# All pieces of the gated layer's weights rounded in the first attention, none in the rotary attention

## The reference, cut to what matters

```python
def nf4_quant_dequant(w):
    flat = w.reshape(-1, 64)
    absmax = jnp.max(jnp.abs(flat), axis=1, keepdims=True)
    normalized = flat / jnp.where(absmax == 0, 1.0, absmax)
    bounds = (NF4_CODE[:-1] + NF4_CODE[1:]) * 0.5
    return (NF4_CODE[jnp.searchsorted(bounds, normalized)] * absmax).reshape(w.shape)
x = x + L0_xattn(norm(x)) ; x = x + L0_ffn(norm(x)) ; ... ; x = x + L2_xattn(norm(x))
h = silu(x @ nf4(w1).T) * (x @ nf4(w2).T) ; x = x + h @ nf4(w3).T    # on norm(x)
```

## Time and profile before

| | before |
|---|---|
| median of 3 runs | 3158.59 us (3151.64 to 3164.6) |
| the profiled execution's own time | 3164.61 us |
| its span | 3162.1 us |
| mean granted TensorE clock | 0.956 |
| busy: TensorE, VectorE, ScalarE, GpSimd | 91%, 63%, 43%, 42% |

### The profile page before, as it was taken

How to read it: one execution, slowest core, us unless ns; L and a number is a source line. 1 busy time by engine, 2 the same in 40 slices (tenths; PEclk the granted TensorE clock), 3 DMA queues, 4 the chain that set the end, 5 groups by cost and what they waited for, 6 DMA issues and landing times. The chain is left out here.

```text
span 3162.1 us, 44768 instructions
## 1 busy us (share of the span) xinstructions
PE 2887.2 (91%) x16404; PEld 2486.6 (79%) x16404; DVE 2001.8 (63%) x3496; ACT 1369.1 (43%) x3381; POOL 1317.0 (42%) x1174
## 2 busy tenths in 40 slices
PE   7999999999876984789999998998999999999967
PEld 6888888888764762578888886887999999999955
DVE  5777777777855777668888875344444444444453
ACT  3656565565611552134444433213444444443520
POOL 6455535554422651455555550003434434443430
PEclk9999999999977996899999999998999999999978
DMA  3112112111121000211111102101000100000000
GB/s 129 49 57 66 58 41 66 60 51 59 39 80 45 11 4 7 70 47 41 44 41 44 32 27 104 51 11 37 28 21 24 31 18 28 28 28 18 18 28 27
DMA packets 77831, 131.85 MB, mean 42 GB/s; under 512 B 10024, under 2 KB 23600, under 8 KB 77232
## 3 DMA queue, kind: packets, MB, share of 16 engines
q1 hardware_dynamic: 68112, 112.10, 11.2%
q10 hardware_dynamic: 9504, 16.91, 1.7%
HBM read 114.23 MB, written 14.75 MB: 41 GB/s over the span
## 5 line engine op out<-in xcount | busy, mean ns | idle before, releaser
L89 PE MATMUL a_pa<-a_wo,a_ot 128*128 128x512 f32 x2304 | 538.5, 391 | 10.4 <-issue 7.5
L89 PEld LDWEIGHTS a_pa<-a_wo,a_ot 128*128 128x128 f32 x2304 | 429.6, 188 | 105.9 <-issue 13.1
L359 DVE SCALAR_TENSOR_TENSOR a_nf_acc<-a_nf_t,a_nf_acc 128x512 f32<-128x512 bf16 (+1 forms) x462 | 403.1, 872 | 46.3 <-ACT a_nf_t L313 15.7
L313 ACT ACTIVATE a_nf_t<-a_nf_w,a_nf_shifts 128x512 bf16<-128x512 f32 (+1 forms) x495 | 321.9, 709 | 178.7 <-DVE a_nf_w L343 149.3
L89 PE MATMUL a_pa<-h_t,a_wqk 128*128 128x512 f32 x1536 | 374.7, 396 | 1.7 <-DVE h_t L770 1.7
L89 PEld LDWEIGHTS a_pa<-h_t,a_wqk 128*128 128x128 f32 x1536 | 283.0, 189 | 56.8 <-DVE h_t L770 1.9
L89 PE MATMUL a_pa<-a_wv,ctx_t 128*128 128x512 f32 x960 | 232.3, 400 | 39.8 <-POOL a_wv L1617 23.9
L89 PEld LDWEIGHTS a_pa<-a_wv,ctx_t 128*128 128x128 f32 x960 | 182.3, 193 | 78.4 <-POOL a_wv L1617 24.8
L89 PE MATMUL a_pa<-ctx_t,a_wqk 128*128 128x512 f32 x960 | 224.5, 390 | 1.2 <-POOL a_wqk L1617 1.0
L89 PEld LDWEIGHTS a_pa<-ctx_t,a_wqk 128*128 128x128 f32 x960 | 179.8, 188 | 39.5 <-POOL a_wqk L1617 2.4
L1006 POOL TENSOR_TENSOR a_prob<-a_prob,a_inv 128x512 f32<-128x512 f32 x128 | 130.6, 1042 | 183.3 <-DVE a_inv L1372 183.3
(11 more groups left out here) (361 smaller groups left out, 6138.5 us busy)
## 6 DMA issues: line engine op xcount, KB each, us to landing
a_raw<-in_a_w SPq DMA_DIRECT2D x288, 256.0 KB, 2.6
a_nf_w<-in_nf ACTq DMA_DIRECT2D x32, 256.0 KB, 2.7
nf_rounded<-a_nf_acc ACTq DMA_DIRECT2D x32, 256.0 KB, 2.0
f_rows<-nf_rounded SPq DMA_DIRECT2D x22, 256.0 KB, 3.0
ctx_kept<-ctx_t SPq DMA_DIRECT2D x1, 4096.0 KB, 17.0
ctx_t<-ctx_kept SPq DMA_DIRECT2D x1, 4096.0 KB
f_cols<-nf_rounded SPq DMA_DIRECT2D x11, 256.0 KB, 3.7
a_ctx_raw<-in_ctxt SPq DMA_DIRECT2D x4, 512.0 KB, 6.8
```

Source lines behind the costliest of these rows:

```text
L89: ins = nc.tensor.matmul(out, lhs(a), rhs(b), start=first and i == 0, stop=last and i == 2)
L313: self.nc.scalar.activation(self.t[:, m % NF4_RING, cols], self.w[:, p % 2, cols], ACT.Identity, bias=self.shifts[:, u - 2:u - 1], scale=s ...
L359: ins = nc.vector.scalar_tensor_tensor(acc, t, c, acc, inner, outer)
```

## The change

`NF4_SIZES` has all 33 pieces and goes to the first attention; the quotas there grow by four units a head on VectorE, and on ScalarE by one after each of the four kept halves. In the rotary attention every trace of the rounding goes: its tiles, its 15 memsets on GpSimd, its loads and stores in ScalarE's queue and its units.

```diff
@@ -236,9 +236,8 @@
 NF4_BLOCKS = 3 * NH2 * D // (P * NF4_BLOCK)
 NF4_UNITS = 18
 NF4_RING = 4
-SIZES0 = [8] * 24
-SIZES2 = [8] * 8 + [2]
-assert sum(SIZES0) + sum(SIZES2) == NF4_BLOCKS
+NF4_SIZES = [8] * 32 + [2]
+assert sum(NF4_SIZES) == NF4_BLOCKS
 
 
 def counted(keys):
@@ -754,9 +753,9 @@
                 if h + 2 < H:
                     for key in (("q", h + 2, 0), ("q", h + 2, 1), ("k", h + 2, 0)):
                         keep(key)
-                        rounding.on_scalar(act, 3 if h % 2 == 0 else 2)
+                        rounding.on_scalar(act, 4 if h % 2 == 0 else 3)
                     keep(("k", h + 2, 1))
-                    rounding.on_scalar(act, 2 if h % 2 == 0 else 6)
+                    rounding.on_scalar(act, 3 if h % 2 == 0 else 7)
             rounding.on_scalar(act, NF4_UNITS * len(rounding.sizes))
             rounding.finish(act)
 
@@ -842,7 +841,7 @@
                     inverse(h + 1, 1)
                 rest_of_o(h, 0)
                 rest_of_o(h, 1)
-                rounding.on_vector(dve, 10 if h % 2 else 13)
+                rounding.on_vector(dve, 14 if h % 2 else 17)
                 for key in bias_outputs(h):
                     add_output(*key)
                     if key[1] % 2:
@@ -1492,7 +1491,7 @@
     return order
 
 
-def rope_attention_stage(nc, x, ident, ctx_t, h_t, where, pieces_in, mask_in, pos_in, iota_in, tables_in, nf4):
+def rope_attention_stage(nc, x, ident, ctx_t, h_t, where, pieces_in, mask_in, pos_in, iota_in, tables_in):
 
 
     st = Stage(nc, "a2")
@@ -1541,7 +1540,6 @@
     top, shift, total, inv = (next_at(n, [P, NB]) for n in ("top", "shift", "total", "inv"))
     space = next_at("space", [P, 11 * NB])
     iota = next_at("iota", [P, DC])
-    rounding = Rounding(nc, st, next_at, *nf4)
 
     pa = st.ps("pa", [P, ROPE_RING, BANK])
     pscore = st.ps("pscore", [P, 2, BANK])
@@ -1567,9 +1565,6 @@
 
     def bank(key):
         return pa[:, (made_count[key] - 1) % ROPE_RING, :]
-
-    def side(step):
-        return (2, 1, 2) if step < 14 else (2, 0, 2)
 
     with nc.Block() as block:
         @block.sync
@@ -1636,7 +1631,6 @@
             norm.rstd_on_gpsimd(nc, pool)
             split(("k", 0))
             split(("k", 1))
-            rounding.set_up_on_gpsimd()
             nc.gpsimd.tensor_scalar(ident_bf[:, :], ident[:, :], 1.0, 0.0, ALU.mult, ALU.add).then_inc(mask_set, 1)
             pool.wait_ge(mask_loaded, 16)
             nc.gpsimd.tensor_scalar(neg[:, :, :], mask[:, :, :], 0.0, NEG, ALU.is_equal, ALU.mult).then_inc(mask_set, 1)
@@ -1827,18 +1821,13 @@
 
             for b in range(NB):
                 keep_values(0, b)
-            act.wait_ge(rounding.shifts_set, 15)
-            rounding.load(act, 0)
-            rounding.load(act, 1)
             for b in range(NB):
                 act.wait_ge(hp_ready, b + 1)
                 nc.scalar.activation(h_t[:, HI, :, b * P:(b + 1) * P], ph[b % 4], ACT.Copy).then_inc(h_hi, 1)
             for b in range(NB):
                 keep_values(1, b)
-                rounding.on_scalar(act, 3)
             exps(0, 0)
             exps(0, 1)
-            rounding.on_scalar(act, side(0)[0])
             for h in range(H):
                 for t in range(2):
                     act.wait_ge(t_ready, 2 * h + t + 1)
@@ -1852,9 +1841,6 @@
                     nc.scalar.activation(ot[:, h % 3, HI, t * BANK:(t + 1) * BANK], ptv[:, t, :], ACT.Copy).then_inc(o_hi, 1)
                 if h + 1 < H:
                     exps(h + 1, 1)
-                rounding.on_scalar(act, sum(side(h)[1:]) + side(h + 1)[0])
-            rounding.on_scalar(act, NF4_UNITS * len(rounding.sizes))
-            rounding.finish(act)
 
         @block.vector
         def _(dve):
@@ -1939,7 +1925,6 @@
             for n in range(1, 4):
                 rotate("k", n, 0)
                 rotate("k", n, 1)
-            rounding.on_vector(dve, 3 * NB)
             for key in (("k", 4), ("k", 5), ("k", 6), ("q", 0), ("k", 7)):
                 rotate(*key, 0)
                 rotate(*key, 1)
@@ -1953,7 +1938,6 @@
                 if h + 1 < H:
                     shifts(h + 1, 0)
                     shifts(h + 1, 1)
-                rounding.on_vector(dve, side(h)[0])
                 if h + 1 < H:
                     inverse(h + 1, 0)
                 if h + 2 < H:
@@ -1962,15 +1946,12 @@
                 rest_of_o(h, 1)
                 if h + 1 < H:
                     inverse(h + 1, 1)
-                rounding.on_vector(dve, side(h)[1])
                 if h + 2 < H:
                     rotate("q", h + 2, 1)
                 for key in rope_outputs(h):
                     add_output(*key)
-                rounding.on_vector(dve, side(h)[2])
             for key in rope_outputs(H):
                 add_output(*key)
-            rounding.on_vector(dve, NF4_UNITS * len(rounding.sizes))
             dve.wait_ge(a_taken, taken_count["o", H // 2 - 1, NB - 1])
     st.close()
 
@@ -3246,7 +3227,7 @@
         free_at = ht_at + 2 * DC * NT * 4
         with nc.sbuf_tensor("h_t0", [P, 2, DC, NT], F32R) as h_t:
             bias_attention_stage(nc, x, ident, ctx_t, h_t, free_at, ins["x"], ins["ident"], ins["ctxt"], ins["a0_w"],
-                                 ins["mask_bool"], ins["pos_bias"], ins["ln_w"], (ins["nf4"], rounded, 0, SIZES0))
+                                 ins["mask_bool"], ins["pos_bias"], ins["ln_w"], (ins["nf4"], rounded, 0, NF4_SIZES))
             ffn0_stage(nc, x, ident, h_t, ins["w_base"], ins["f0_side"], ins["lora_b"], ins["b_base"], ins["b_router"],
                        ctx_t, ctx_kept)
         patch_attention_stage(nc, x, ident, ins["ctx"], ins["mask_f"], ins["a1_wqk"], ins["a1_wv"], ins["a1_wo"],
@@ -3265,8 +3246,7 @@
                 ffn1_stage(nc, x, h, ident_bf, ins["f1_w"], ins["f1_scale"], ins["f1_bias"])
         with nc.sbuf_tensor("h_t1", [P, 2, DC, NT], F32R) as h_t:
             rope_attention_stage(nc, x, ident, ctx_t, h_t, (ctx_at, ht_at, free_at), ins["a2_w"], ins["mask_i"], ins["pos"],
-                                 ins["iota"], ins["rope"],
-                                 (ins["nf4"], rounded, sum(SIZES0), SIZES2))
+                                 ins["iota"], ins["rope"])
             ffn2_stage(nc, x, ident, h_t, rounded_rows, ctx_t, ctx_kept)
             latent_attention_stage(nc, x, ident, ctx_t, h_t, free_at, ins["a3_w"], ins["a3_norm"])
             ffn3_stage(nc, x, ident, h_t, ins["f3_a"], ins["f3_b"], ins["f3_router"], ins["f3_keys"])
```

## The result

| | before | after |
|---|---|---|
| median | 3161.44 us (3151.64 to 3164.6, 4 runs) | 3278.15 us (3272.7 to 3279.29, 4 runs) |
| ratio | | 1.0369, 95% interval 1.0353 to 1.0386 |
| span, mean granted clock | 3162.1 us, 0.956 | 3277.2 us, 0.943 |

The kernel became 3.7% slower. The forecast of 3238 us had the sign and the place right, and was 40 us short; the time lies 6 us above its range. Lines of the kernel after are one lower than before in the first attention (the scores are L632, the keeps L700).

What follows compares the result with a forecast made beforehand. The prediction took TensorE to bound the kernel before and VectorE the first attention's heads after. +68 +21 -10 = +79 on 3164.6 us gave 3243.6, less 6.0 for the median 3238 us; range 3188 to 3272 (80%).

Steps and rivals of the forecast that it cites:

- (a): VectorE's rounding in the first attention: a unit costs 0.77 us undisturbed, 0.965 in an even head, 1.31 beside `wv` splits.
- (b): First attention's heads: VectorE's own length makes a pair 59.0 us against 54.1; 13 pairs and head 0 give +68.
- (c): Even heads' scores wait 1.5 to 7 us for ScalarE's late keep of `k`; this pays (b), adding nothing.
- (d): End of the first attention: units left after head 29 delay `rest_of_o(31)`, the last additions and the last store, +21.
- (e): Rotary attention: waits freed by taking its rounding out, -10, bounds 0 and -28.
- The checks named beforehand: Heads: pair near 59 us, VectorE 85% or more, TensorE under 92%; rotary heads 15.8 us, VectorE near 65%.
- Rival 1: VectorE's spare quarter takes all added units, the pair stays 54.1 and the rotary stage gives 28: 3141 us, 4%.
- Rival 2: Milder: the additions' idle time and smoother rhythm take most, a pair grows 1.5 to 2 us: 3193 us, 18%.
- Rival 4: The work moves and nothing is seen, time within 16 us: 4%.
- Rival 3: Late keeps in even heads and bank waits in odd ones add, with half clock behind them: +114, 3273 us, 20%.
- SBUF: two separate sides: If the shared ports lock exclusively, added units cost 0.77 us each where GpSimd rests; sum some 25 us less.

Runs made afterwards that it cites:

- experiment 3: Kernel before with other piece counts, first plus rotary attention: 28 + 4.25 took 3220.9 us, 24 + 0 took 3147.8, 20 + 0 took 3121.8 (pair 52.6).
- keep first: Kernel after, with ScalarE's rounding units from between the two halves of `k` put behind the second half: 3276.7 us.
- experiment 1: ScalarE's rounding units between the halves of `k` moved behind the second half: 3276.7 us in the kernel after, 3155.6 us in the kernel before.
- experiment 2: Unused filler matmuls in TensorE's waits: kernel after, at the scores, 12 took 3272.2 us, 24 took 3269.8; with `k` kept sooner, at the outputs, 3270.8.
- weigh first: Kernel after with `k` kept ahead of ScalarE's rounding, and the weighing and its drain put ahead of the value tiles and their keeps: 3291.1 us.

## Why the prediction was short

(a) *Unit prices held.* The mean instruction is 875 ns, where the forecast priced a unit at 0.965 us in the even head and 1.31 beside `wv` splits. The segments of units sum to 33.6 us a pair, where the forecast had 34.65 for the same (18.15 + 16.5).

(b) *This step failed, in two of its terms and in what it concluded for the kernel before.* VectorE's segments of a pair, mean of 13, after: shift to the end of `rest_of_o` 9.54 and 9.77 us where (b) took 8.25 twice, from one odd head; additions, up to the next shift, 9.05 where it took 7.8; units 1.0 less. That is 61.95 instead of 59.0. The 7.8 left out the 0.55 us wait in front of that shift, and with it the head chosen, 8.36 us, was among the shortest of before, whose mean was 9.9. The segment could be read beforehand too: in twelve of the thirteen even heads of before this segment was 9.4 us long, and the timeline of before shows why, a wait of 2.52 and not of 1.07 us as in the row chosen:
```profile
672.85 0.69 DVE L777 TENSOR_TENSOR a_prob<-a_pscore,a_bias 128x512 f32<-128x512 f32 x1 [0.55 <-PE a_pscore L633]
...
680.74 1.52 DVE L795 TENSOR_TENSOR a_ot<-a_ptv,a_ot 128x512 fp32r<-128x512 f32 x2 [2.52 <-ACT a_ot L752]
```
"No waiting for TensorE is left in it" was read off the odd head 25, whose shifts start late and whose `ot` is waited for only 1.07 us; it was false of the even ones. The same shortfall made "before, the same sum is about 50, below TensorE's" wrong, and with it the 4 us a pair of cover that the forecast gave the added units. There was none: TensorE's own pair is 52.6 (experiment 3) and the kernel before stood 1.5 above it. Eight units without cover at 0.98 us are 7.85 a pair, +102 instead of +64. VectorE's idle time, 23% of the pairs of before, was no reserve: 129 of its 164 us were waits for ScalarE and TensorE, and after the change they were 135. How the pair splits into segments depends on the order of the queues: in keep first the odd heads' segment is 8.05 us, as forecast, but the additions are 10.0, and the pair is 61.7 all the same. Only the even heads' 9.5 us are there in both; why the rest comes back elsewhere is not shown.

(c) *Held.* The scores' wait for `k` is in 14 heads, 64.1 us, the forecast's 40 or more; and it is where (b) is paid, not added: experiment 1 took it away and the bank waits took its place. The banks were waited for 7 times, 15.4 us in all.

(d) *Held*, +21.1 for +21, and nearly term by term: measured from the scores of head 27, `rest_of_o(31)` ends 15.1 us later (forecast 5 + 10), the last addition 17.9 (17), the next stage 21.1 (21). (e) *Held*, -9.3 for -10 in the rotary stage's stretch; its own terms sum to 9.3 and were rounded up. Experiment 3 gives 13 for taking the nine pieces out.

In spans the forecast was +79 and the measurement +115.1, 36 us short, and (b) has nearly all of it: 104.8 us in the heads where it had 68. The other 4 of the 40 us are in how the medians lie to the profiled executions: 6.0 below it before, 1.1 below it after.

The checks named beforehand: rotary heads with VectorE near 65%, yes; TensorE under 92% in the heads, 90.0%; VectorE at 85% or more, no, 78%: its waits did not shrink. A rotary head at 15.8 us, yes, 15.86.

*The rivals.* Rivals 1, 2 and 4 fell with the pair: a slope of 0.98 us a unit from a kernel already above TensorE's length left no room for a rhythm that takes the units in. Rival 3 named 3273 us, 5 off, but its mechanism, waits that add up with the clock on top, is not what the runs show: the waits replace each other (experiment 1), and of the 36 us of slower matmuls the fillers gave back 6 to 8 (experiment 2). The Trainium skill, page "TensorE: Matmul & The Clock Gate", section "HAM oscillation — how this bites in real kernels", describes the clock's pattern that came, 16 stretches at the lower level in the heads; the runs add that it cost little of its own here. The Trainium skill, page "SBUF — State Buffer", section "SBUF: two separate sides", was given 25 us in the forecast. The forecast's own terms give half of that: eight units at 0.77 us are 6.2 us for the 7.2 in (b), 1.0 a pair or 13 us. The unit segments came out 1.0 us a pair below the forecast; no run here separates the ports' part in that, and it did not decide.

## What to carry to other kernels

A share of idle time need not be a reserve where an engine hands work around in a loop with others. Measure the floor before forecasting: take work off in one kernel and see whether the period still falls. Where it does (54.1 to 52.6 us here), expect added units to cost their full length, here 0.98 us each. And take a latency that occurs in every period from all periods, even and odd apart, not from one row: 8.25 for 9.54 and 9.77 us and 7.8 for 9.05, less the 1.0 us that the units fell short, are 2.95 us a pair, 38 us in 13 pairs.

## What the runs showed that was not expected

A wait of an engine that is released late can be moved to another place without any gain in time: the kernel after had 64.1 us of it at the scores, keep first 54.4 at the output banks, weigh first 66.9 at the weighing. The first two took the same time, the third 0.4% more.

The clock's lower level can be nearly free where another engine sets the period: between 85 and 34 us of half clock lie 8 us of time.
